# Five edits to a three-stage transformer kernel: first job in halves, mask load, last gate, bank hand-over, last expert

## The reference

```python
# 1: embedding and a 4-layer encoder, 16 heads of 16
h = emb[x] + pos
for l in range(4):
    y = layer_norm(h); q, k, v = y @ Wq + bq, y @ Wk + bk, y @ Wv + bv
    h = h + softmax(q k^T / 4) v @ Wo + bo
    h = h + relu(layer_norm(h) @ w1 + b1) @ w2 + b2
h = layer_norm(h)
# 2: segment attention, windows of 128, 16 heads of 64, 16 memory keys, causal mask
h = h + attend(rmsnorm(layernorm(h)) @ w_qkv, mask) @ w_out
# 3: gate (top 2 of 16 experts, capacity 320), experts and 2 shared experts
x = layernorm(h); logits = x @ gate_w; topi = top_k(softmax(logits) + gate_b, 2)
for e in range(16):                      # at most 320 tokens each, by largest weight
    out[idx_e] += silu(x_e @ w1_e) * (x_e @ w3_e) @ w2_e * weight_e
h = h + out + mean(shared experts of x)
```

## Time and profile before

| | |
|---|---|
| median of 3 runs | 2026.21 us (2025.81 to 2026.54) |
| profiled execution, its own time | 2026.1 us |
| its span in the trace | 2024.3 us |
| TensorE busy | 1994.4 us (99%) |
| VectorE, ScalarE, GpSimd busy | 64%, 51%, 11% |
| mean granted TensorE clock | 0.998 of full |

### The profile page before, as it was taken

One profiled execution on the slowest core, in us unless ns is written; L12 is line 12 of the kernel. 1 busy time (PEld: TensorE's weight loads), 2 busy tenths in 40 slices (PEclk: granted clock), 3 DMA queues, 4 the chain that ended last, 5 costly groups with the idle time before them and its releaser, 6 DMA issues. The chain is left out here.

```text
span 2024.3 us, 42309 instructions
## 1 busy us (share of the span) xinstructions
PE 1994.4 (99%) x16486; PEld 1666.4 (82%) x16486; DVE 1297.9 (64%) x3339; ACT 1034.7 (51%) x3526; POOL 215.8 (11%) x251
## 2 busy tenths in 40 slices
PE   7999999999999999999999999999999999999999
PEld 5888888888888888888888887788888888877776
DVE  6777777767767767767768764777776656322332
ACT  5666666666666666666666661555454521111111
POOL 1101000000000000000000000000000000434444
PEclk9999999999999999999999999999999999999999
DMA  2110000200000400000000002300000100035542
GB/s 93 39 50 9 4 2 2 71 2 2 1 2 2 161 2 2 1 2 2 1 2 2 1 2 68 123 1 1 1 1 1 63 1 21 23 90 158 170 136 66
DMA packets 27203, 69.84 MB, mean 35 GB/s; under 512 B 9920, under 2 KB 17825, under 8 KB 23680
## 3 DMA queue, kind: packets, MB, share of 16 engines
q1 hardware_dynamic: 18432, 59.42, 8.7%
q0 software_dynamic: 6400, 5.63, 1.1%
q10 hardware_dynamic: 2176, 2.10, 0.3%
HBM read 61.16 MB, written 17.40 MB: 39 GB/s over the span
## 5 line engine op out<-in xcount | busy, mean ns | idle before, releaser
L575 ACT ACTIVATE probs<-bank,nmax 128x256 f32<-128x256 f32 x1024 | 471.2, 480 | 233.0 <-DVE nmax L750 232.4
L750 DVE TENSOR_REDUCE nmax<-bank 128x2 f32<-128x512 f32 x512 | 322.1, 681 | 50.6 <-PE bank L406 50.6
L419 PE MATMUL bank<-ident,probs 128*128 128x128 f32 x2048 | 273.0, 276 | 1.7 <-DVE pts L758 1.1
L419 PEld LDWEIGHTS bank<-ident,probs 128*128 128x128 f32 x2048 | 229.6, 141 | 49.9 <-issue 33.7
L451 PE MATMUL bank<-yT,weights 128*128 128x256 f32 x1024 | 236.8, 380 | 0.0
L584 ACT ACTIVATE pts<-bank 128x512 f32<-128x512 f32 x256 | 157.0, 613 | 153.7 <-PE bank L419 152.6
L463 PE MATMUL bank<-weights,aT 128*128 128x256 f32 x1024 | 231.7, 380 | 2.2 <-ACT probs L575 1.9
L575 ACT ACTIVATION_READ_ACCUMULATOR probs<-bank,nmax 128x1 f32 x1024 | 216.6, 211 | 0.0
L463 PEld LDWEIGHTS bank<-weights,aT 128*128 128x128 f32 x1024 | 192.3, 190 | 27.6 <-issue 2.8
L758 DVE COPY pts<-bank 128x512 f32<-128x512 f32 x256 | 175.8, 687 | 46.2 <-PE bank L419 42.3
L451 PEld LDWEIGHTS bank<-yT,weights 128*128 128x128 f32 x1024 | 187.7, 191 | 21.2
(11 more groups left out here) (228 smaller groups left out, 2969.6 us busy)
## 6 DMA issues: line engine op xcount, KB each, us to landing
wqkv<-in_experts SPq DMA_DIRECT2D x16, 1024.0 KB, 5.0
weights<-in_wtok SPq DMA_DIRECT2D x4, 2048.0 KB, 10.4
wqkv<-in_experts SPq DMA_DIRECT2D x16, 512.0 KB, 3.7
expert_rows<-xT_all SPq DMA_DIRECT2D x10, 546.0 KB, 16.2
xrows<-expert_rows SPq DMA_DIRECT2D x16, 273.0 KB, 3.2
weights<-in_wtok SPq DMA_DIRECT2D x3, 1024.0 KB, 4.7
wqkv<-in_wqkv SPq DMA_DIRECT2D x1, 3072.0 KB, 17.9
weights<-in_shared SPq DMA_DIRECT2D x1, 3072.0 KB, 11.6
```

What stands on the lines that cost most here:

```text
L419: last = pe.transpose(g[:, (NT * x + kb) * P:(NT * x + kb + 1) * P], p[:, x, kb * P:(kb + 1) * P], ident[:])
L575: last = nc.scalar.activation(probs[u % 8][:, x, :], g[:, x * S:(x + 1) * S], ACT.Exp, bias=nmax[j % 2][:, col:col + 1], accum_out=rsum[j ...
L750: nc.vector.tensor_reduce(nmax[j % 2][:, col:col + 2], g[:].rearrange("p (x s) -> p x s", x=2), AX.X, ALU.max, negate=True).then_inc(s_max, 1)
```

## The change

1. **Start.** Three VectorE instructions in place of five make the gather's indices. The first two tiles have semaphores of their own, and `first_stats` works tile by tile. Two `idle` matmuls ahead of the first transposes go. Queries and keys of job 0 are made by halves of features (`first_half`), each half with its own bank and its own writing out (`first_q_out`, `first_k_out`); the second half of the keys stands behind the first scores, and two `idle` matmuls behind the values.
2. **Mask.** `mask` is loaded in the encoder's queue, with other constants of the second stage, and VectorE waits for no load at the boundary.
3. **Last gate.** `LAST_X`, `LAST_LG` and `KEYS_AT` are one unit later.
4. **Hand-over.** GpSimd, in place of ScalarE, hands the six banks over.
5. **Last expert.** `down(14)` stands after the second `up` unit of expert 15, not after the fourth, and VectorE's `add(14)` follows it.

```diff
-        use((0, "yT"), 4), use((0, "q"), 7), use((0, "k"), 5)
+        use((0, "yT"), 4), use((0, "q", 0), 7), use((0, "k", 0), 5), use((0, "q", 1), 6), use((0, "k", 1), 4)
...
-            sp.wait_ge(s_gather[0], 16 * NT)
+            sp.wait_ge(s_gather[0], 16 * (NT - 1))
             sp.dma_start(weights[0][:, 0:1024], io["wtok"][0, :, 0:1024]).then_inc(s_w[0], 16)
             sp.dma_start(qmask[:], io["qmask"]).then_inc(s_w[0], 16)
...
-            evacuated(sp, (0, "k"))
+            evacuated(sp, (0, "k", 1))
...
+            sp.dma_start(mask[:], io["mask"]).then_inc(s_w2c, 16)
...
-                                            bass.IndirectOffsetOnAxis(ap=idxu[:, j:j + 1], axis=0)).then_inc(s_gather[j // NT], 16)
+                                            bass.IndirectOffsetOnAxis(ap=idxu[:, j:j + 1], axis=0)).then_inc(s_first if j == 0 else s_gather[j // NT], 16)
...
+            def first_half(name, n, m):
+                if (name, m) == ("q", 0):
+                    evacuated(pe, (0, "yT"))
+                    pe.wait_ge(s_w[0], 16 * NLOAD)
+                g = acquire(pe, (0, name, m))
+                for k in range(KD):
+                    last = pe.matmul(g[:, m * S:(m + 1) * S], wqkvo[0][:, n, k, m * P:(m + 1) * P],
+                                     yT[0][:, k, :], start=(k == 0), stop=(k == KD - 1))
+                filled(last, (0, name, m))
...
-                if c == 0:
+                qt, ch = c // 2, c % 2
+                if j == 0 and qt == 0:
+                    evacuated(pe, (0, "q", ch))
+                    evacuated(pe, (0, "k", ch))
+                if j > 0 and c == 0:
...
-            pe.wait_ge(s_gather[0], 16 * NT)
-            idle(2)
+            pe.wait_ge(s_gather[0], 16 * (NT - 1))
+            idle(1)
             pe.wait_ge(s_var[0], 1)
-            idle(1)
-            pe.wait_ge(s_sd[0], 1)
             idle(1)
             y_T(0)
             idle(1)
-            feature_major(0, "q", 0)
-            feature_major(0, "k", 1)
+
+            first_half("q", 0, 0)
+            first_half("k", 1, 0)
+            first_half("q", 0, 1)
...
+                    if (j, c) == (0, 0):
+                        first_half("k", 1, 1)
...
+                        if j == 0:
+                            evacuated(pe, (0, "q", 1))
+                            idle(2, 1)
...
+            def first_k_out(m):
+                g = take(act, (0, "k", m))
+                release(nc.scalar.activation(kT[0][:, m, :], g[:, m * S:(m + 1) * S], ACT.Identity,
+                                             bias=cols[0][:, C_BK + m:C_BK + m + 1]), (0, "k", m))
...
-            k_out(0)
+            first_k_out(0)
...
+                        if (j, c, n) == (0, 0, 0):
+                            first_k_out(1)
...
-            step.up(nc.vector.tensor_copy(idxf[:], idx[:]))
+            step.up(nc.vector.tensor_scalar(idxn[:], idx[:], 0.0, float(V), ALU.is_lt, ALU.mult))
             step.wait(dve)
-            step.up(nc.vector.tensor_scalar(idxn[:], idxf[:], 0.0, float(V), ALU.is_lt, ALU.mult))
+            step.up(nc.vector.tensor_tensor(idxf[:], idx[:], idxn[:], ALU.add))
             step.wait(dve)
-            step.up(nc.vector.tensor_tensor(idxf[:], idxf[:], idxn[:], ALU.add))
-            step.wait(dve)
-            step.up(nc.vector.tensor_scalar(idxn[:], idxf[:], 0.0, float(V - 1), ALU.max, ALU.min))
-            step.wait(dve)
-            nc.vector.tensor_copy(idxu[:], idxn[:]).then_inc(s_idx, 1)
+            nc.vector.tensor_scalar(idxu[:], idxf[:], 0.0, float(V - 1), ALU.max, ALU.min).then_inc(s_idx, 1)
...
+            def first_stats():
+                for i in range(NT):
+                    dve.wait_ge(s_gather[0] if i else s_first, 16)
+                    step.up(nc.vector.tensor_tensor(h[:, 0, i, :], h[:, 0, i, :], pe_sb[:, i, :], ALU.add))
+                    after_held()
+                    step.up(nc.vector.bn_stats(stats[0][:, i, :], h[:, 0, i, :]))
+                    after_held()
+                    last = nc.vector.bn_aggr(mv[0][:, i, :], stats[0][:, i, :])
+                    if i + 1 < NT:
+                        step.up(last)
+                last.then_inc(s_var[0], 1)
...
+            def first_q_out(m):
+                if m == 0:
+                    dve.wait_ge(s_w[0], 16 * NLOAD)
+                g = take(dve, (0, "q", m))
+                for x in range(STRIP):
+                    last = nc.vector.tensor_scalar(qm[0][:, x, m, :], g[:, m * S:(m + 1) * S],
+                                                   cols[0][:, C_BQ + m:C_BQ + m + 1], qmask[:, x:x + 1],
+                                                   ALU.add, ALU.mult)
+                release(last, (0, "q", m))
...
-            positions(0)
-            stats_of(1, 0)
+            first_stats()
...
-            q_out(0)
+            first_q_out(0)
+            first_q_out(1)
...
-    LAST_X, LAST_LG = EARLY + 2, EARLY + 3
-    KEYS_AT = EARLY + 6
+    LAST_X, LAST_LG = EARLY + 3, EARLY + 4
+    KEYS_AT = EARLY + 7
...
-            sp.dma_start(mask[:], io["mask"]).then_inc(s_const, 16)
...
-                    pe.wait_ge(s_const, 32)
+                    pe.wait_ge(s_const, 16)
...
-                if G == 0 and j == 0:
-                    dve.wait_ge(s_const, 32)
...
+        units_ahead = lambda e: HT if e + 1 < E else HT // 2
...
+            for n in range(6):
+                i = (first_bank + n) % 6
+                bank_left(pool, i)
+                nc.gpsimd.memset(scratch[:, i:i + 1], 0.0).then_inc(s_free[i], 1)
...
-                for i in range(HT):
+                for i in range(units_ahead(e)):
                     up(e, i)
                 if e:
                     down(e - 1)
                 if e + 1 < E:
                     rows_T(e + 1)
-                for i in range(HT, 2 * HT):
+                for i in range(units_ahead(e), 2 * HT):
...
-            for n in range(5):
-                hand_over(n)
             rows_out(0)
-            hand_over(5)
...
-                    if m == HT // 2:
+                    if m == units_ahead(e) // 2:
```

More of the change, by code:

```diff
@@ L133, in step, with embed_and_encoder @@
             last.then_inc(self.s_yn, 1)
-def embed_and_encoder(nc, io, h, ident, weights, wqkv, wout, norm, normab, gamma, pmk, w_yT, w_qT0, w_kT0):
+def embed_and_encoder(nc, io, h, ident, weights, wqkv, wout, norm, normab, gamma, pmk, mask, w_yT, w_qT0, w_kT0):
     JOBS = L * B
@@ L226, in embed_and_encoder @@
         s_gather = [sem(f"s_gather{s}") for s in range(B)]
+        s_first = sem("s_first_tile")
         s_h = sem("s_h")
@@ L397, in scores @@
                     return
-                if c == 0:
+                qt, ch = c // 2, c % 2
[3 more added lines that the diff above has]
+                if j > 0 and c == 0:
                     evacuated(pe, (j, "q"))
                     evacuated(pe, (j, "k"))
-                qt, ch = c // 2, c % 2
                 gs = [acquire(pe, (j, "S", 4 * c + n)) for n in range(4)]
@@ L616, in second_out @@
                 if n == "yT":
-                    act.wait_ge(s_w2c, 48)
+                    act.wait_ge(s_w2c, 64)
                     for k in range(KD):
@@ L811, in second_norm @@
                 if n == 2:
-                    dve.wait_ge(s_w2c, 48)
+                    dve.wait_ge(s_w2c, 64)
                 norm.step(nc, dve, step, scratch[:, 8:], h, normab, s, n)
@@ L885, in _, with attention_and_shared @@
                                 second_k_out(u[2])
-def attention_and_shared(nc, io, h, ident, weights, wqkv, wout, norm, normab, gamma, pmk, w_yT, w_qT0, w_kT0,
+def attention_and_shared(nc, io, h, ident, weights, wqkv, wout, norm, normab, gamma, pmk, mask, w_yT, w_qT0, w_kT0,
                          loads, XS, half_of, sem, block):
@@ L904, in attention_and_shared @@
         sb = lambda name, shape, dt=F32: ctx.enter_context(nc.sbuf_tensor(name, shape, dt))
-        mask = sb("mask", [P, 1, KEYS2])
         pmv = sb("pmv", [P, INNER])
@@ L1981, in silus @@
                 release(nc.scalar.activation(silu[n % 4][:], g[:, 0:CAP], ACT.Silu), u)
-            def hand_over(n):
-                i = (first_bank + n) % 6
-                bank_left(act, i)
-                nc.scalar.activation(scratch[:, i:i + 1], half_of[:, 0:1], ACT.Copy).then_inc(s_free[i], 1)
-            for n in range(5):
-                hand_over(n)
             rows_out(0)
-            hand_over(5)
             for e in range(E):
@@ L2058, in build @@
         pmk = sb("pmk", [P, CT, 1, PM])
+        mask = sb("mask", [P, 1, KEYS2])
         norm = SecondNorm(sb, sem)
@@ L2069, in build @@
         loads = ExpertLoads(io, XS, [wqkv[:, a, :] for a in range(2)], sb, sem)
-        embed_and_encoder(nc, io, h, ident, weights, wqkv, wout, norm, normab, gamma, pmk, w_yT, w_qT0, w_kT0)
+        embed_and_encoder(nc, io, h, ident, weights, wqkv, wout, norm, normab, gamma, pmk, mask, w_yT, w_qT0, w_kT0)
```

(2 more changed lines are left out.)

## The result

| | median us | runs | ratio to the kernel before, 95% |
|---|---|---|---|
| before | 2026.21 | 2025.81 to 2028.18 | |
| after | 2015.91 | 2015.47 to 2017.28 | 0.9948 [0.9936, 0.9959] |

The medians are 10.3 us apart (the runs of before are five here). The profiled execution of after was the slowest of its five, 2017.28 us (span 2015.5), so between the two profiles lie only 8.8 us. The 1.4 us that it has over its own median are part of what follows.

What follows compares the result with a forecast made beforehand. TensorE, busy 99% of the span, was taken to bound the kernel, so only its waits, low clock and tail give time. 3.0 + 2.9 + 1.66 + 0.95 + 1.7 + 0.64 = 10.8, 2026.2 - 10.8 = 2015.4 us; range 2013.9 to 2018.2.

Steps and rivals of the forecast that it cites:

- Start, 3.0: Job 0, from gather to scores: shorter chain brings the second scores at 23.0 and not 26.00, 3.0 us; bounds 2.3 and 3.4.
- queries begin at about 12.94 + 1.1 = 14.05: Start of job 0: qmask there at 12.94, first query pass 1.1 us later, at 14.05 and not 15.55.
- the load lands no earlier: Rival for the start: qmask stays at 13.36, queries begin 0.42 us later than summed, total 2015.8; chance 0.14.
- The halves' cost: VectorE's position sum at the start: by formula two halves cost 0.16 us more in total, hidden in the second tile's wait.
- Mask, 2.9: Boundary to the attention: with the mask there, VectorE's first sum begins at 1254.8, all behind moves 2.9 us; bounds 2.4, 3.2.
- the lower clock just behind costs nothing now and gives nothing back, since TensorE then waits for VectorE: Behind the boundary (transposes at 1264): the lower clock changes nothing in the mask's gain, as VectorE's chain bounds there.
- Last gate, 1.66: TensorE's 1.74 us wait for `x_all` before the last `x_T` is filled by a moved unit: 1.66 us; bounds 1.3 and 1.8.
- Hand-over, 0.95: Start of the experts: TensorE no longer waits for ScalarE's bank hand-over and begins at 1795.0: 0.95 us; bounds 0.7 and 1.2.
- Clock behind it, 1.7: Behind the experts' start: with a shorter gap the clock holds instead of 0.56: 1.7 us more; bounds 0 and 1.9.
- the rival at 0.24: The clock falls anyway behind the experts' start and 1.7 us stay lost: 2017.1; chance 0.24.
- Last expert, 0.64: End of the kernel: earlier `down(14)` brings fetches and the last scatter forward, to 2021.15: 0.64 us; bounds 0 and 1.0.
- the "6.1" among its signs: Sign at the end: last scatter 6.1 us behind the start of `down(15)` and not 6.9.

Runs made afterwards that it cites:

- e9: The changed kernel with two matmuls nobody reads (512 and 256 columns) in TensorE's gaps behind the boundary, the same edit as e6 run again: median 2015.97 us.
- e10: The changed kernel with the two fillers behind the boundary, and four idle matmuls in place of five at the start: median 2015.57 us.
- e6: The changed kernel with two matmuls nobody reads (512 and 256 columns) in TensorE's gaps behind the boundary, first time: median 2016.56 us.
- e11: The changed kernel with the two fillers behind the boundary, and first weights and qmask loaded at once, not behind the second gathered tile: median 2016.04 us.
- e7: The changed kernel with ScalarE handing banks over as before, and one unread 512-column matmul in TensorE's gap before expert 0's transposes: median 2017.85 us.
- e1: The changed kernel with the whole start edit undone (first job, index instructions, tile semaphores, idle matmuls as before): median 2020.16 us.
- e2: The changed kernel with the mask loaded behind the boundary, as before the change: median 2021.87 us.
- e8: The changed kernel once more, with no edit: median 2016.97 us.
- e12: The changed kernel with the two fillers behind the boundary, four idle matmuls at the start, and qmask loaded ahead of the gathers: median 2015.71 us.

## Why the prediction was right, point by point

The forecast, 2015.4 us, was met to 0.5 us (2015.91), inside its own range. The terms:

- **Start, 3.0: 2.35**, just above the lower bound. From the queries to the second scores it was exact: 8.95 us forecast (14.05 to 23.0), 8.94 measured. The failed step is "queries begin at about 12.94 + 1.1 = 14.05": they began at 14.44. Two terms of it were off. The load was to come 0.42 earlier with the indices. They came 0.30 earlier (2.89 for 3.19) and the tile as late as before, so the load was issued at 9.42 (9.46 before) and `qmask` was there at about 13.2 (3.8 us). And the idle matmuls ended at 12.66, not 12.06: the first began at 4.30 and not 4.08, and by the weight loads its passes stood 0.86 us apart until 8.73, not only until 7.66, and 0.43 soon after. In this profile the second term ended last: ScalarE's write of `yT` at 13.37 waited for the transposes. In e9 and e10 it was the first. The rival "the load lands no earlier" forecast the same 0.42 us, so its time came true while its mechanism was only one of the two. In e6 the tile was there by 8.33 and `qmask` issued at 8.52, 0.9 us sooner than in e9, yet ScalarE had it only at 13.18, 0.32 sooner. With e11 this speaks for transfers that delay one another, without showing it. It agrees with the Trainium skill ("DMA: Bandwidth & Descriptors", "Issuing engines are not separate DMA queues"), by which DMAs of all engines run on the same 16 and interleave. The other 0.27 us are lost at 170 us.
- The halves' cost: a 128x256 sum took 0.43 us, and two are 0.17 more than the 0.69 of one whole. The estimate by the Trainium skill's formula ("VectorE: DVE Perf Modes", "The TRN2 errata — SBUF-src ops pay a fixed extra latency per instruction") had 0.16, so the trace agrees. It did not count, since the first lay in the wait for the second tile, as the prediction said.
- **Mask, 2.9: 2.88 with the clock up (17.12 to 14.24), 1.73 where it falls.** The step "the lower clock just behind costs nothing now and gives nothing back, since TensorE then waits for VectorE" held for before only. With the mask early the fall comes in the value passes, where TensorE bounds: VectorE waits 0.81 us for the scores of group 2 then. The term's own bounds (2.4 and 3.2) did not cover 1.73; only the range of the whole did.
- **Last gate, 1.66: 1.74.** It took over the full wait, and keys kept their 0.36 us.
- **Hand-over, 0.95: 1.15**, inside its bounds. As the prediction put it, VectorE bounds: its memsets end at 1788.40, its copy starts at 1788.31, 1.33 us behind the last shared unit (forecast 1.41), and TensorE 0.68 behind that (0.75).
- **Clock behind it, 1.7: 1.69**, with the clock at 1.00 there in all eleven profiles with GpSimd's hand-over and in the one with the gap filled, and fallen in both with the long gap. The most doubtful term came out to 0.01 us; the rival at 0.24 fell, and e7 shows that filling the gap is enough to hold the clock.
- **Last expert, 0.64: 0.63.** The last scatter stands 6.28 us behind the last product. The sum in the text gives 6.27; the "6.1" among its signs is a slip.

The sum with the clock up and without the odd 0.48 us is 2.35 + 2.88 + 1.74 + 1.15 + 1.69 + 0.63 = 10.4 us, where the medians are 10.3 apart; forecast 10.8 (its terms add to 10.85). The total was nearer than the terms: the start was 0.65 too high, hand-over and last gate 0.28 too low. And there is luck in it: where the clock falls at the boundary the same sum is 9.3 us, and the text had no term for that. The median agrees with the sum for executions in which it holds there.

## What to carry to other kernels

Where TensorE must wait for a microsecond or more, try matmuls that nobody reads in the wait: at both places here (gaps of 1.5 and of 1.3 and 0.6 us) they cost nothing and the clock stayed up. A gap may lie at the edge, where the clock falls in one execution and not in the next; then the spread of the runs is the sign, and one profile of either kind misleads by the price of the fall. Removing a wait ahead of such a place moves the fall into other work, so ask what bounds there then. Before a load is moved, see whether it is what the wait is for, or another that shares its semaphore. And a transfer asked for earlier need not be there earlier: the second tile, asked for 0.29 us earlier, came when it had before.

## What was not expected of the hardware

- The clock fell at 1260 to 1268 us in five profiles and held in two with the same code at that place. The Trainium skill ("TensorE: Matmul & The Clock Gate", "Part 1: The HAM clock gate") says that the watch on TensorE's activity is free-running and doesn't reset when a kernel starts; a fall that depends on the execution agrees with that, but no run here tests it.
- At 52 us (55 in e1), in the products with values L450 (L436 in e1, L449 in e2), TensorE paused twice for 0.3 us with "issue" as the cause in the profiles of e1 to e8, and not in those of before, after and e9 to e12. With the new start it is 1228.98 to 1229.10 us from the second scores to the boundary in the former and 1228.09 to 1228.11 in the latter. The cause is open; e1 to e8 ran on two chips and the others on different ones.
- SP took 1.63 us to issue a load of 8 KB (`iota`) in e2; before, the same issue took 0.43 us.
